# Nine early expert tiles filled by the first four batches, and the transition's calls written out anew: a cross-attention and mixture-of-experts layer on one core

## The reference

```python
x = x + jnp.tanh(g_xattn[0]) * xattn(_layernorm(x), ctx_1024, w_q, w_kv, w_out, b_out)   # 16 heads of 64
x = x + jnp.tanh(g_ffn[0])   * ffn(_layernorm(x), W1, W2, Wr)
# ffn: logits = x @ Wr.T; softmax over 8 experts; the best 2, their weights scaled to sum 1
#      h = silu(x @ W1[e].T) (256 -> 1024);  y = h @ W2[e].T (1024 -> 256);  out = sum of gate * y
```

## Time and profile before

| what | value |
|---|---|
| runs | 528.67, 528.88, 530.03 us (median 528.88) |
| profiled execution | 530.4 us, its span 528.7 us |
| mean granted TensorE clock | 0.983 of full speed |
| busy in the span | PE 92%, DVE 69%, ACT 70%, POOL 70% |
| chain that ended last | PE 66%, POOL 12%, DVE 9%, ACT 5%, issue 5%, DMA 3% |

### The profile page before, as it was taken

The page is one execution under the profiler, slowest core; times in us unless marked ns, Lnnn a source line. Parts: engine busy times, 40 slices in busy tenths (PEclk is TensorE's granted clock), DMA queues, the critical chain, the costliest instruction groups (busy, mean ns, idle before and its releaser), DMA issues.

```text
span 528.7 us, 17694 instructions
## 1 busy us (share of the span) xinstructions
PE 486.9 (92%) x6692; PEld 436.4 (83%) x6692; DVE 363.8 (69%) x866; ACT 371.2 (70%) x577; POOL 369.9 (70%) x414
## 2 busy tenths in 40 slices
PE   2889689999999999999688999989999999999993
PEld 2877568888888878888468899979999999999993
DVE  5799899898988989998887757553344443444431
ACT  1788989999899989988764577544555655556551
POOL 5369779798999999899968766564554645455432
PEclk9999989999999999999989999998999999999998
DMA  7953416154360725325073638886888888788712
GB/s 289 398 195 95 167 38 204 51 185 140 99 208 34 243 67 182 124 95 195 24 268 110 255 118 303 251 254 150 260 226 245 241 226 265 212 256 239 211 22 31
DMA packets 35061, 94.87 MB, mean 179 GB/s; under 512 B 4507, under 2 KB 24475, under 8 KB 27645
## 3 DMA queue, kind: packets, MB, share of 16 engines
q1 hardware_dynamic: 25812, 82.79, 45.2%
q0 software_dynamic: 8592, 10.81, 11.9%
q10 hardware_dynamic: 576, 0.14, 0.1%
HBM read 74.45 MB, written 19.28 MB: 177 GB/s over the span
## 4 chain that ended last, share of the span: by engine, by line
PE 66%; POOL 12%; DVE 9%; ACT 5%; issue 5%; DMA 3%; POOLq 0%; SPq 0%; ACTq 0%; DVEq 0%
PE st_bank L1707 20%; PE j_bank L1707 15%; PE o_bank L1707 14%; PE j_bank L1852 4%; POOL pT L618 3%; POOL stage L663 3%; PE max_pair L1908 2%; PE j_bank L1713 2%; PE st_bank L1929 2%; POOL table L637 2%; PE j_bank L1811 2%; DMA stage<-in_w 2%; PE max_pair L1970 1%; DMA w2s<-in_wq 1%; PE j_bank L1876 1%
## 5 line engine op out<-in xcount | busy, mean ns | idle before, releaser
L1541 DVE SCALAR_TENSOR_TENSOR hT<-hf,h_scale,hT 128x512 f16<-128x512 f32 x78 | 58.9, 758 | 87.2 <-ACT hT L1016 87.1
L1707 PE MATMUL st_bank<-xsT,w_tile 128*128 128x128 f16 x1872 | 113.3, 221 | 2.1 <-DVE xsT L1535 1.4
L1707 PEld LDWEIGHTS st_bank<-xsT,w_tile 128*128 128x128 f16 x1872 | 109.6, 99 | 3.0 <-DVE xsT L1535 1.6
L730 POOL DMA_INDIRECT out<-yt,row_of x39 | 62.7, 1607 | 57.0 <-DVE yt L1550 42.3
L1010 ACT ACTIVATE hf<-st_bank,z_scale 128x512 f32<-128x512 f32 x78 | 52.9, 678 | 45.2 <-PE st_bank L1707 39.2
L618 POOL TENSOR_TENSOR pT<-pT 120x512 f16<-120x512 f32 x64 | 77.3, 1223 | 7.3 <-ACT pT L884 7.1
L1707 PE MATMUL o_bank<-w2s,hT 128*128 x600 | 69.7, 273 | 0.3 <-DVE yt L1550 0.3
L1016 ACT ACTIVATE hT<-hf,h_scale 128x512 f16<-128x512 f32 x78 | 56.3, 722 | 10.5 <-PE o_bank L1707 4.2
L1707 PEld LDWEIGHTS o_bank<-w2s,hT 128*128 128x128 f16 x600 | 57.6, 98 | 7.1 <-issue 0.8
L883 ACT ACTIVATE pT<-st_bank,exp_bias,logit_scale 120x512 f32<-120x512 f32 x64 | 50.0, 781 | 14.0 <-PE st_bank L1932 12.7
L663 POOL TENSOR_SCALAR stage<-stage,upw 128x512 f32<-128x512 f32 x32 | 56.5, 1766 | 4.1 <-ACT w_hi L983 4.1
(11 more groups left out here) (226 smaller groups left out, 1022.7 us busy)
## 6 DMA issues: line engine op xcount, KB each, us to landing
w_tile<-w_split SPq DMA_DIRECT2D x39, 1024.0 KB, 6.3
stage<-in_w SPq DMA_DIRECT2D x16, 1024.0 KB, 5.1
w_split<-w_hi SPq DMA_DIRECT2D x8, 512.0 KB, 2.8
w_split<-stage SPq DMA_DIRECT2D x8, 512.0 KB, 3.8
out<-x SPq DMA_DIRECT2D x17, 128.0 KB, 3.2
xin<-in_x SPq DMA_DIRECT2D x8, 256.0 KB
w2s<-in_wkv SPq DMA_DIRECT2D x2, 1024.0 KB, 11.9
xres<-in_x SPq DMA_DIRECT2D x16, 128.0 KB, 2.1
```

The lines of the kernel that those rows point to most:

```text
L730: pool.indirect_dma_start(out=out[0:rows], out_offset=bass.IndirectOffsetOnAxis(row_of[:, t:t + 1], 0), in_=yt[t % XG][:], in_offset=None, ...
L1541: nc.vector.scalar_tensor_tensor(out=hT[par][:, 1, 4 * a:4 * a + 4, :], in0=hf[par][:, 512 * a:512 * a + 512].rearrange("p (c n) -> p c n" ...
L1707: ins = pe.matmul(out, lhs[i](a), rhs[i](c), start=(i == 0 and a + c == 0), stop=(i == n - 1 and a == 1))
```

## The change

`EARLY_B` goes from 5 to 4, so `EARLY` from 13 to 9: tiles 9 and up are now late. With it all early steps (`count_tiles`, `find_rows`, `find_T`, `row_ids`, `tile_experts`) come one iteration sooner, and FE moves in the job lists. The loops end with iteration 5, and everything behind is written out call by call on PE, DVE, ACT and POOL, in a new order (SP's loop stays). ScalarE's `hidden` no longer waits for `tile_gates` but for the second step of `tile_scales` (`units_done`). `add_wait` is made in place of a separate `prior`, and `turn_over` lies elsewhere in SBUF. The spare matmuls become 14 and 18; the last expert's four low halves of w2 are all made by VectorE, where GpSimd made two.

```diff
-EARLY_B = 5
+EARLY_B = 4
...
-PRODUCT_ORDER = (("Awq", 4), ("Q3", 2), ("X2T", -1), ("Q1", 2), ("LG", -1), ("FE", -2), ("Ka", 2), ("Vb", 1), ("OT0a", 0),
-                 ("MT1", 1), ("OT1b", 0), ("Kb", 2), ("A3", 2), ("OT0b", 0), ("Q2", 2), ("RK", -1), ("PJ1", 0),
+PRODUCT_ORDER = (("Awq", 4), ("Q3", 2), ("X2T", -1), ("Q1", 2), ("LG", -1), ("Ka", 2), ("Vb", 1), ("OT0a", 0),
+                 ("MT1", 1), ("OT1b", 0), ("FE", -2), ("Kb", 2), ("A3", 2), ("OT0b", 0), ("Q2", 2), ("RK", -1), ("PJ1", 0),
...
-                act.wait_ge(tables_done, 1 if isinstance(t, int) and t < EARLY else 2)
+                act.wait_ge(units_done, 1 if isinstance(t, int) and t < EARLY else 2)
```

GpSimd, behind the loop:

```diff
+            p_low(6, 2, 1)
+            norm2_factors(5)
+            scatter(4, 1)
+            p_low(6, 3, 0)
+            p_low(6, 3, 1)
+            split_low(7, 0, 1)
+            split_low(7, 0, 3)
+            p_low(7, 0, 0)
+            p_low(7, 0, 1)
+            tile_gather(7, 0)
+            tile_gather(7, 1)
+            p_low(7, 1, 0)
...
+            scatter(7, 0)
+            scatter(7, 1)
+            tile_add(7, 2)
+            find_rows(7, 1)
+            tile_add(7, 3)
+            tile_gather(7, 9)
```

VectorE, in the loop that stays (so that the early count, now of batch 3, comes in iteration 5), and behind it:

```diff
                 norm_o(p, 2, 0)
+                count_tiles(p - 2, 0, 0)
+                count_tiles(p - 2, 0, 1)
+                count_tiles(p - 2, 0, 2)
                 row_max(p + 1, 2)
...
                 max_rows(p + 1, 1)
+                row_ids(p - 2, 0)
+                tile_experts(p - 2, 0)
...
+            norm_o(7, 1, 1)
+            add_residual(6, 0)
+            tile_scales(7, 0, 0)
+            tile_low(7, 0)
+            norm_o(7, 2, 0)
+            tile_scales(7, 0, 1)
+            tile_low(7, 1)
...
+            split_low(7, 1, 0)
+            split_low(7, 1, 1)
+            split_low(7, 1, 2)
+            split_low(7, 1, 3)
```

TensorE, in the loop that stays, and behind it:

```diff
                 o_T(p, 1, 1)
+                find_T(p - 2, 0)
                 k_product(p + 2, 1)
...
+            out_product(6, 1, 1)
+            col_scores(7, 3)
+            out_product(6, 0, 0)
+            out_product(6, 0, 1)
+            values(7, 1, 1)
+            tile_T(7, 0)
+            tile_T(7, 1)
+            spare("OT1a", 7, 14)
+            values(7, 2, 0)
+            spare("OT1a", 7, 18)
+            tile_up(7, 0, 0)
+            o_T(7, 1, 0)
...
+            ranks(7)
+            tile_down(7, 2)
+            tile_up(7, 4, 0)
...
+            tile_up(7, 7, 1)
+            find_T(7, 1)
+            tile_up(7, 8, 0)
+            tile_T(7, 9)
+            tile_down(7, 6)
+            tile_up(7, 8, 1)
+            tile_up(7, 9, 0)
+            tile_T(7, 10)
+            tile_down(7, 7)
+            tile_up(7, 9, 1)
+            tile_down(7, 8)
```

482 lines of the change are left out of this document (300 added, 182 removed).

## The result

The changed kernel takes 550.92 us (median of 4; 549.13 to 554.09) beside 529.45 for the kernel before in the same comparison: 1.0423 times, 95% interval 1.0365 to 1.0482, so slower by 21.5 us. The profiled execution took 549.19 us, its span 547.5: 18.8 over the profiled one of before. To follow where they arise I set the clock to zero at the rank products of batch 3, ahead of which nothing is changed (212.25 us before, 212.67 after), and read the starts of four later marks from the timeline of TensorE. All later sums are differences of such starts. Medians are of all executions, while the ratios leave out those in a slower state, so that they are not quotients of the medians.

A forecast was written before the change was run, and what follows sets the result against it. TensorE bounds attention; the lever is batch 6's transition. Terms -1.7 - 3.4 + 5.1 gave 0.0, plus 1.3 for operations beside GpSimd and 1.0 for the clock: +2.3 on 530.4, 531.2 us against the median; range 524.5 to 534.5.

The forecast's parts named there:

- Early count, +5.0 at ranks(4): Batch 5's iteration: the count makes VectorE late and Kb waits for its new bank, ranks(4) 5.0 us later.
- 0 to 2.6 for those held: Early count in batch 5: up to six scalar forms slowed beside GpSimd's tensor work, 0 to 2.6 us, +1.3 taken.
- Kb, +2.1 and FE, +0.4: Batch 5's ring of three banks: Kb needs MT1(6)'s bank, about +2.1 us; FE itself adds 0.4.
- row_ids and tile_experts, nothing more: Batch 5: five short instructions, about 0.9 us, ahead of work that waits for Kb anyway, adding nothing.
- Batch 6 gives it back, 0 at ranks(5): Batch 6: count and scales gone, some 10 us of VectorE; GpSimd leads and ranks(5) comes level, near 274.3.
- the clock, which I had entered with 1.0: Batch 6, behind the wait at values(6,3,0): products may run at the lower level, 0 to 1.9 us, +1.0 taken.
- Batch 7, -1.7 at ranks(7): Batch 7: fewer fillers and moved tables bring tile 0's first product 2.4 us sooner, ranks(7) 1.7 us sooner.
- Old stall, -3.4: Waits around the transposes of tiles 10 and 11, and slow products behind them, all go: -3.4 us.
- T9, +5.1: Tile 9's transpose: TensorE waits 3.5 us for the gather's rows, and 1.64 us for the clock is added.
- The rival of an early landing: At T9: gathered rows land early, only 0.8 us of the +5.1 stays; 524.6, or 525.9 us; chance 0.22.
- the estimate of 2.3 us: Gather's landing at T9 by the skill page's fit for 128 KB; the wait would be 1.4 us.
- that batch 5 keeps its pace: Batch 5: VectorE and Kb take only 2.5 us of lag to ranks(4); 526.4 us; chance 0.13.

The follow-up runs named there:

- b1: Changed kernel with the early count at the place in batch 5's iteration that it had in batch 6's before; 543.93 us, 1.0316 to the kernel before.
- b4: Changed kernel with GpSimd's scatter(4,1) ahead of norm2_factors(5) again; 547.41 us, 1.0373 to the kernel before.
- c1: New order with thirteen early tiles by five batches, tile 0's low half moved ahead of its expert scales on VectorE; 528.16 us, 1.0014 to the kernel before.
- a4: Changed kernel's new order alone, with thirteen early tiles by five batches and the early steps back in batch 6; 530.91 us, 1.0042 to the kernel before.
- f3: The kernel before, unchanged, profiled again; 528.31 us, 0.9988 to the kernel before.
- a2: Changed kernel with find_T behind Kb and row_ids and tile_experts behind k_low(7,1); 549.76 us, 1.0427 to the kernel before.
- f1: Changed kernel, count at its old place in the iteration, find_T behind Kb, scatter(4,1) first, tile 9 later, tile 0's low half before scales; 539.38 us, 1.0194.
- d2: New order by five batches, tile 0's low half first, copy of maxima, weight scales and norm_o(6,2,0) ahead of the count's later stages; 531.27 us, 1.0066.
- a1: Changed kernel with the early count cut in three stages set later on VectorE, find_rows one split later; 546.07 us, 1.0332 to the kernel before.
- a3: Changed kernel with tile 9's transpose behind down6 and up(8,1), its ScalarE and VectorE parts moved along; 546.35 us, 1.0358 to the kernel before.
- d1: Changed kernel, count's late stages behind norm_o(5,2,0), find_T behind Kb, scatter(4,1) first, tile 9 later, tile 0's low half before scales; 540.46 us, 1.0244.

## Why the prediction went as it did

The side was right (slower as forecast, and at T9 and Kb for the reasons given), the size was not: +21.5 us against +2.3, far over the range's end of 534.5.

*Early count, +5.0 at ranks(4): this step failed.* Three things in it. First, the term of 3.4 us for the 17 operations, with 0 to 2.6 for those held: they took 6.8, so that the holding was 3.4, over its upper bound. I had up to six scalar forms at 0.43 each, from the mean of the six scales; five operations were slow, by 0.42 to 0.90 each, a scan and a subtraction among them. The trace of before had this already. Right behind the one that I read, at 254.68, stands another that ends within 0.02 us of the two p_low of the earlier trace rows (256.55), and of the scales the one at 276.02, which has two inputs, took 1.08 us:

```profile
255.49 1.08 DVE L1318 TENSOR_SCALAR upw<-pw 128x2 int32<-128x2 int32 x1
```

Second, the place: I had q_product(7,3) wait for o_low(5,1,0); one place earlier values(5,3,0) waits for norm_o(5,2,1), since all values share one bank. Taken off the 5.53 us, the 3.4 leave 2.1, near the 2.5 that I had; by this estimate the misread place alone would have cost little, which no run shows. Third, no term for the clock stood in this step. A wait of 5.5 us brought it down here, and with Kb's dip it cost about 4.8 (3.3 of the 4.01, and 1.53). b1, where one operation is held and the clock stays, comes to +5.4, by waits of 0.87, 2.56 and 1.72 us: about what the step had.

The Trainium skill's page "SBUF — State Buffer", section "Who interferes with whom", says that VectorE and GpSimd share a pair of ports which one of them holds for a whole instruction, and that VectorE's tensor_scalar and forms with two inputs in SBUF can be shut out by it. The ends that coincide above, and the reductions with one input that stay at 0.16 us, agree; the operation of 0.17 us at 226.97, with two such inputs beside GpSimd's scaling, does not, and neither does the end at 226.94 in the middle of that scaling.

*Kb, +2.1 and FE, +0.4:* 1.72 and 0.5. *row_ids and tile_experts, nothing more:* the five operations took 2.2 us (248.45 to 250.69) where I had 0.9, two of them ending with a p_low; what that cost is not told apart by a run.

*Batch 6 gives it back, 0 at ranks(5): failed with the first.* The chain was read rightly, norm2_factors(5), scatter, p_low, then values(6,3,0), and b4 confirms it. It gave back 1.42 and not 5 or more, since it begins with VectorE's statistics and so moved with VectorE (263.61, where I had 255.0). From there to ranks(5) I had 19.3 us; it took 22.4. About 1.9 of the difference is the clock, which I had entered with 1.0: from values(6,3,0) to ranks(5) it takes 14.89 us here and 13.00 in b4, where these products run at full clock. The rest is not told apart.

*Batch 7, -1.7 at ranks(7): failed by its second half.* up(0,0) comes 1.48 us sooner behind ranks(5) (forecast 2.4), though it waits 2.33 for the low half of tile 0, which I had put at 285.5 without asking what stands ahead of it: the scales begin 9.1 us behind ranks(5), and not 6.9, behind a normalization that waits 2.94 us for its values. Then waits of 0.92 and 0.96 and the clock behind them take 2.95 back. c1 shows that wait alone to be 1.5.

*Old stall, -3.4:* a4, which has no late tile there, is 1.96 us quicker behind ranks(7), and its two new waits, 0.87 for a gating and 0.58, make up the rest: right against this profile, but for these two. The 1.64 us of slow products in it were luck of one execution, though: f3, the same kernel without them, is only 0.40 us slower there than a4.

*T9, +5.1:* the mechanism was right, the term too small by 1.8: the wait was 4.73 (3.5 forecast), the clock 2.16 (1.64). T9 began 5.67 us after the gather's issue began, where I had taken 4.4 and at most 5.3. The view of the tile has the gathers there land 2.8 to 3.6 us after their issue; what lies between that and the start is not told. The DMA engines are busy 0.94 of the time there, at 348 GB/s (the window from 350 us above); whether that delays the rows no run shows.

```profile
DMA to landing us min/median/max: 2.8/3.2/3.6
```

The rival of an early landing (under 2.5 us) fell by either reading, and with it the estimate of 2.3 us from the Trainium skill's page "DMA: Bandwidth & Descriptors", section "Anatomy of one DMA — SWDGE (gpsimd) path".

Of the rivals, none came; that batch 5 keeps its pace was furthest off. What stays open: why the same wait brings the clock down in one execution and not in another; and why the single gains of a2, b4 and b1 do not add up in f1 (39.72 and 28.98 us, where b1 has 36.12 and b4 26.67), beyond the clock in it.

## What to carry to other kernels

Before small VectorE operations are moved, lay the two timelines of VectorE and GpSimd side by side at the new place: here a chain of operations of 0.2 us doubled where GpSimd worked on large tensors (6.8 us), and showed its own length where GpSimd issued DMAs and worked on two elements (3.4). In a stage where TensorE is busy without a gap, price a wait twice, once as a wait and once as slow products behind it, and give the second its own range. A chain on an engine "with time in hand" gives lateness back only from the point at which it doesn't itself wait for the late engine.

## What the runs showed of the hardware that was not expected

A held operation need not be released between two successive operations of GpSimd: on two elements it lasted 2.93 us (c1), and on 128x8 2.69 (d2), across both p_low; both began during the issue of a scatter. In d2, first VectorE, then GpSimd:

```profile
255.38 2.69 DVE L1528 TENSOR_SCALAR small<-iota,small 128x8 f32<-128x8 f32 x1
```

```profile
255.76 2.27 POOL L617 TENSOR_TENSOR pT<-pT 120x512 f16<-120x512 f32 x2
```

GpSimd's scaling of 128x512 does not hold to its end what begins with it: in eight profiles (after and before, a1, a2, a3, b4, d1, f3) a small operation of VectorE that begins within 0.1 us of the start of this scaling, which takes 1.57 us, ends 0.70 to 0.72 us after that start; the fifth slow operation of the count, at 226.30, is one of them. The granted clock is not a function of the wait alone: behind 1.41 us at tile 10 part of the products ran at 1.2 GHz in one execution of the kernel before (48 in 4.48 us) and all at 2.4 in another (2.85), behind 2.56 and 2.49 us at the V product they ran at 2.4 and at 1.2, and behind 2.33 us at up(0,0) 24 products took 1.51 us in the changed kernel and 2.74 in b1. T9 began 5.67 us after the issue of its gather, and 5.88 in a3 (issue at 354.15, T9 at 360.03 behind a wait that ends with the gather). Both are longer than either table search of the earlier trace rows took to land, though by the view of the tile the gathers there landed in 2.8 to 3.6 us (3.9 in a3).
